# A top-k threshold search on two engines: three counting rounds for four, from a first guess computed on TensorE

## What is computed

```python
x = x + tanh(g_xattn) * attention(layernorm(x), ctx, ctx, Wq, bq, Wk, bk, Wv, bv, Wo, bo)
x = x + tanh(g_ffn) * ffn_fp8(layernorm(x), kernel, scales, bias)
# attention, 16 heads, d = 16:
Q = (q @ Wq.T + bq).reshape(b, h, s, d)      # a head is 16 tokens x 16 feature groups
scores = einsum('bhqd,bhkd->bhqk', Q, K) / sqrt(d)
topk_scores, topk_idx = top_k(scores, 64)    # 64 of 256 keys per row
probs = softmax(topk_scores)
out = einsum('bhqk,bhqkd->bhqd', probs, gather(V, topk_idx)) @ Wo.T + bo
```

## Time and profile before

| | |
|---|---|
| median of 3 runs | 3270.99 us (3270.64 to 3272.13) |
| the profiled execution | 3268.81 us, of it 3266.9 us span |
| ACT busy | 2730.3 us, 84% |
| DVE busy | 2691.6 us, 82% |
| PE busy | 1780.4 us, 54% |
| POOL busy | 966.1 us, 30% |
| tiles selected again by `settle` | 7 |

### The profile page before, as it was taken

How to read it: one execution, slowest core, us unless ns; L and a number is a source line. 1 busy time by engine, 2 the same in 40 slices (tenths; PEclk the granted TensorE clock), 3 DMA queues, 4 the chain that set the end, 5 groups by cost and what they waited for, 6 DMA issues and landing times.

```text
span 3266.9 us, 51511 instructions
## 1 busy us (share of the span) xinstructions
PE 1780.4 (54%) x7952; PEld 950.5 (29%) x7952; DVE 2691.6 (82%) x11883; ACT 2730.3 (84%) x9638; POOL 966.1 (30%) x1174
## 2 busy tenths in 40 slices
PE   3245555555465555455556556564556556454555
PEld 2122233332233233232323333332233223232222
DVE  1678888888888888888888888888888888888884
ACT  1888888998788898797889998988798788997983
POOL 5122223233222233232233223333223233232112
PEclk8567677777677777776667777767676767777777
DMA  4223332223333223331233333223333133331211
GB/s 70 38 43 60 49 47 52 52 49 63 52 52 54 45 49 63 52 55 34 48 64 56 60 48 56 48 48 64 53 49 55 33 62 61 55 54 33 40 24 46
DMA packets 451902, 166.43 MB, mean 51 GB/s; under 512 B 245616, under 2 KB 451440, under 8 KB 451520
## 3 DMA queue, kind: packets, MB, share of 16 engines
q1 hardware_dynamic: 451136, 162.38, 28.4%
q0 software_dynamic: 384, 0.33, 0.1%
HBM read 102.57 MB, written 59.24 MB: 50 GB/s over the span
## 4 chain that ended last, share of the span: by engine, by line
DVE 36%; ACT 30%; issue 17%; PE 14%; DVEq 2%; POOL 1%; ACTq 0%; DMA 0%; SPq 0%; POOLq 0%; another core or an unknown queue 0%
ACT act_junk L880 22%; DVE masked L1151 5%; DVE score_sb L1047 4%; PE ps_o L731 4%; DVE following L1157 4%; DVE masked L1146 3%; ACT unfit L891 3%; ACT pT_sb L900 2%; PE ps_a L684 2%; DVE X L1083 2%; PE ps_b L675 2%; PE ps_e L712 1%; PE ps_a L686 1%; DVE chord L1115 1%; PE ps_e L716 1%
## 5 line engine op out<-in xcount | busy, mean ns | idle before, releaser
L880 ACT ACTIVATE act_junk<-score_sb,X 128x256 int8<-128x256 f32 x3840 | 1892.1, 503 | 211.3 <-DVE X L1121 183.2
L712 PE MATMUL ps_e<-qs,ks 99*128 99x256 bf16 x1024 | 348.2, 350 | 1321.7 <-ACT pT_sb L900 1321.7
L731 PE MATMUL ps_o<-pT_sb,v_aug 128*32 128x256 f32 x2048 | 766.4, 514 | 0.5 <-ACT pT_sb L900 0.5
L880 ACT ACTIVATION_READ_ACCUMULATOR act_junk<-score_sb,X 128x1 f32 x3840 | 755.0, 197 | 0.0
L891 ACT ACTIVATE unfit<-score_sb,thr 128x256 bf16<-128x256 f32 x1024 | 463.1, 504 | 218.0 <-DVEq L1241 214.6
L1047 DVE TENSOR_SCALAR_CACHE_REDUCE score_sb<-ps_s 128x256 f32<-128x256 f32 x1024 | 418.8, 415 | 142.1 <-PE ps_s L698 140.0
L712 PEld LDWEIGHTS ps_e<-qs,ks 99*128 99x128 bf16 x1024 | 121.9, 119 | 1403.6 <-ACT unfit L891 1199.5
L1146 DVE TENSOR_SCALAR_CACHE_REDUCE masked<-score_sb,X 128x256 f32<-128x256 f32 x1024 | 426.3, 472 | 19.1 <-DVE x_res L1294 8.4
L1157 DVE MAX8 following<-masked 128x8 f32<-128x256 f32 x1024 | 357.7, 409 | 1.7 <-issue 0.7
L540 POOL CAST split<-proj 128x512 bf16<-128x512 f32 x64 | 48.0, 750 | 1042.8 <-ACT proj L866 1027.2
L716 PE MATMUL ps_e<-dropb,unfit 128*128 128x128 bf16 x2048 | 355.9, 273 | 0.0
(11 more groups left out here) (158 smaller groups left out, 3332.8 us busy)
## 6 DMA issues: line engine op xcount, KB each, us to landing
rows<-q_scr SPq DMA_DIRECT2D x192, 128.0 KB, 5.1
rows<-k_scr SPq DMA_DIRECT2D x192, 128.0 KB, 5.0
o_scr<-o_sb SPq DMA_DIRECT2D x128, 128.0 KB, 2.7
q_scr<-split SPq DMA_DIRECT2D x32, 384.0 KB, 2.7
k_scr<-split SPq DMA_DIRECT2D x32, 384.0 KB, 2.7
x_in<-in_x SPq DMA_DIRECT2D x32, 256.0 KB, 3.1
ctx_sb<-in_ctx SPq DMA_DIRECT2D x32, 256.0 KB, 2.7
v_scr<-proj SPq DMA_DIRECT2D x32, 256.0 KB, 5.8
```

Source lines behind the costliest of these rows:

```text
L712: nc.tensor.matmul(ps_e[:, n % 2, kc * TOK:(kc + 1) * TOK], ks[u][:, h, 8 * kc:8 * kc + 8, :].rearrange("d j t -> d (j t)"), qs[u][:, h, : ...
L731: ins = nc.tensor.matmul(ps_o[32 * c:32 * c + 32, half * TOK:(half + 1) * TOK], v_aug[p][:, 2 * h + kc, :], pT_sb[:, n % 2, kc * TOK:(kc + ...
L880: ins = nc.scalar.activation(act_junk[:, t, :], score_sb[:, slot, t, :], ACT.Sign, scale=-1.0, bias=X[slot % 2][:, 0, t:t + 1], accum_out= ...
```

## The change

It alters four things together.

1. **First guess.** DVE sums the keys and their squares (`sum_keys`; the squares come from POOL), PE turns the sums into a mean and a mean square for each head and dimension (`key_moments`), DVE makes weights of them (`weigh_keys`), PE multiplies the queries with these weights (`gauss`, 16 small matmuls for each group), ACT squares and copies the result (`evacuate_gauss`), and DVE takes X = mean + 0.6745 x deviation. The square root is an approximation on the bits.
2. **Rounds.** Three instead of four. ACT counts all 16 tiles.
3. **Finals.** Of 16 tiles, 4 (tiles 4, 5, 10, 11) are counted by ACT (`final_counts`, behind its guide counts); DVE masks those four one by one (L1309) rather than counting them and masking them four at a time.
4. **Heads per round.** With three rounds, ACT does heads (0, 1, 2), (3, 4, 5), (6, 7) in them, and DVE copies the same heads' scores.

The core of the diff, shortened:

```diff
-GUIDES = 4
-ACT_TILES = 15
+GUIDES = 3
-START = 0.25
-SLOPE = 0.0040 / 2
+START = 0.6745
+SLOPE = 0.0115 / 2
+WIDE = ((0, 1, 2, 3), (6, 7, 8, 9), (12, 13, 14, 15))
+NARROW = ((4, 5), (10, 11), ())
+HEADS = ((0, 1, 2), (3, 4, 5), (6, 7))
...
+                nc.gpsimd.tensor_tensor(rest[:], proj[1][:], proj[1][:], ALU.mult).then_inc(s_sq, 1)
...
+            def final_counts(i, slot, r, counted):
+                act.wait_ge(s_fin, FINAL * i + 1)
+                act.wait_ge(s_cnt, counted)
+                for t in NARROW[r]:
+                    ins = nc.scalar.activation(act_junk[:, t, :], score_sb[:, slot, t, :], ACT.Sign, scale=-1.0,
+                                               bias=X[slot % 2][:, 0, t:t + 1], accum_out=final_count[:, t:t + 1])
+                ins.then_inc(s_fc, 1)
+            def evacuate_gauss(i):
+                act.wait_ge(s_gs, i + 1)
+                act.wait_ge(s_st, at(3 * i))
+                act.wait_ge(s_fin, at(FINAL * (i - 2)))
+                both = ps_b[:, 0:(D + 1) * GT].rearrange("p (t d) -> p t d", d=D + 1)
+                nc.scalar.activation(gauss_sq, both[:, :, 0:D], ACT.Square)
+                nc.scalar.copy(gauss_mean[:], both[:, :, D]).then_inc(s_ge, 1)
...
             def start_thresholds(i, slot):
                 dve.wait_ge(s_copied, GH * i + GH)
                 carry(dve)
+                dve.wait_ge(s_ge, i + 1)
+                carry(dve)
...
-                nc.vector.tensor_scalar(x[:, 0, :], mx[:, slot, :], START, None, ALU.mult).then_inc(s_thr, 1)
+                nc.vector.tensor_reduce(variance[:], gauss_sq, AX.X, ALU.add).then_inc(s_st, 1)
+                root(sd[:], variance[:]).then_inc(s_st, 1)
+                nc.vector.scalar_tensor_tensor(x[:, 0, :], sd[:], START, gauss_mean[:], ALU.mult, ALU.add).then_inc(s_st, 1)
...
+                    for k, t in enumerate(narrow):
+                        nc.vector.scalar_tensor_tensor(masked[:, k, :], score_sb[:, slot, t, :], X[slot % 2][:, 0, t:t + 1],
+                                                       score_sb[:, slot, t, :], ALU.is_le, ALU.mult).then_inc(s_fin, 1)
...
-                nc.vector.tensor_tensor(unsure_b[:], s64[:], s65[:], ALU.is_le).then_inc(s_flag, 1)
+                nc.vector.scalar_tensor_tensor(unsure_b[:], s65[:], 0.0, s64[:], ALU.max, ALU.is_ge).then_inc(s_flag, 1)
...
                         for jh in range(2):
                             next(ending, None)
-                            if has(1) and not last:
-                                copy_scores(i + 2, fresh, 2 * r + 1, jh)
+                            if not last:
+                                copy(HEADS[r][2], jh)
                             next(steps, None)
```

More of the change, by code:

```diff
@@ L151, in build @@
         listed_i = sb("listed_i", [1, GT + 1], I32)
+        gauss_sq = place[:].bitcast(BF16)
+        gauss_mean = sb("gauss_mean", [P, GT])
+        variance = sb("variance", [P, GT])
+        spread = [sb(f"spread{k}", [P, GT]) for k in range(2)]
+        pick_dims = sb("pick_dims", [P, D])
+        key_sums = sb("key_sums", [P, 2, EC, NJ])
+        key_stats = sb("key_stats", [D, 2 * NJ])
+        key_var = sb("key_var", [D, NJ])
+        gauss_w = sb("gauss_w", [D, NJ, D + 1], BF16)
         ones_c = sb("ones_c", [P, 1])
@@ L820, in batch @@
                             out_project(b - 2, 2 * b + 1)
+                        if has(1) and n == 5:
+                            gauss(b + 1, (u + 1) % OPS, g, 2 * b + 6 if has(2) else 2 * NB,
+                                  2 * b + 4 + 2 * g if has(2) else 2 * NB)
+                        if has(2) and (g, n) == (1, 7):
+                            key_moments(b + 2)
             schedule(pe, batch)
@@ L946, in batch @@
                             guide_counts(2 * b + g + 1, (2 * p + g + 1) % RING, r)
-                        for n in (2 * r, 2 * r + 1):
+                        if NARROW[r]:
+                            final_counts(2 * b + g, 2 * p + g, r, GUIDES * (2 * b + g + 1) + (r + 1 if guided else 0))
+                        if has(1) and (g, r) == (0, 0):
+                            evacuate_moments(b + 1)
+                        if has(1) and r == GUIDES - 1:
+                            evacuate_gauss(2 * (b + 1) + g)
+                        for n in HEADS[r]:
                             if mixes:
@@ L962, in batch @@
                                 evacuate_ffn(b - 3)
+            evacuate_moments(0)
+            for g in range(2):
+                evacuate_gauss(g)
             for r in range(GUIDES):
@@ L1155, in final_tiles @@
                 carry(dve)
-                for k, t in enumerate(tiles):
+                for k, t in enumerate(wide):
                     nc.vector.max(following[:, t, 1:], masked[:, k, :]).then_inc(s_fin, 1)
+                yield
+                base += 2 * QUARTER + 1
+                if narrow:
+                    dve.wait_ge(s_fin, base)
+                    carry(dve)
+                    for k, t in enumerate(narrow):
+                        nc.vector.scalar_tensor_tensor(masked[:, k, :], score_sb[:, slot, t, :], X[slot % 2][:, 0, t:t + 1],
+                                                       score_sb[:, slot, t, :], ALU.is_le, ALU.mult).then_inc(s_fin, 1)
@@ L1299, in _ @@
             front_moments(1)
+            sum_keys(0)
+            weigh_keys(0)
             for i in range(2):
@@ L1335, in batch @@
                             convert_unsure(i - 1)
-                        if has(1):
-                            copy_scores(i + 2, fresh, 2 * r, 1)
-                        next(finals, None)
+                        copy(HEADS[r][0], 1)
+                        next(finals)
                         if r == 0 and mixes:
                             settle(i - 1, mixed)
-                        last = r == GUIDES - 1
+                        if has(1) and (g, r) == (0, 0):
+                            weigh_keys(b + 1)
+                        if has(2) and (g, r) == (1, 2):
+                            sum_keys(b + 2)
+                        next(finals)
+                        copy(HEADS[r][1], 0)
+                        copy(HEADS[r][1], 1)
+                        next(finals, None)
                         if last and has(1):
-                            for jh in range(2):
-                                copy_scores(i + 2, fresh, 2 * r + 1, jh)
                             start_thresholds(i + 2, fresh)
```

217 lines of the change are left out of this document (161 added, 56 removed).

## The result

The changed kernel takes 3369.54 us (median of 4, 3366.05 to 3371.54) against 3271.25 (median of 4) before: ratio 1.0299, 95% interval 1.0281 to 1.0317, so 98 us or 3.0% slower. Forecast was 3343 us, range 3285 to 3405. The profiled execution took 3371.54 us.

What follows compares the result with a forecast made beforehand. Each round was taken as bound by the later of two paths, ACT's counts and heads or DVE's finals, extras and update. From the 3271.0 us median, -19 for the rounds and +91 for settled tiles gave 3343 us, range 3285 to 3405.

Steps and rivals of the forecast that it cites:

- the five signs: In the changed profile: 15 settling runs, ACT 78 us, L1000 waiting 4 us, score waits over 140.0, clean batch 92.5 to 94.
- Settled tiles: Tiles settled after the rounds: 15 in 12 groups by float32 replay, 179 us against 88 for 7 before, +91 us.
- What the engines are spared: Work per batch: ACT 6.8 us less, DVE 5.1 us less; the ceiling of the gain, the order deciding how much shows.
- The first new wait: ACT's copy of four mixed heads waits for PE's mixing stage behind head 3: 2.1 us, 4.2 for the two groups.
- The second: Score copy ahead of the write of X, rounds 0 and 1, waits on PE; value projection 7.1 us in first group's round 0.
- The six rounds: A batch's rounds, each between ACT's first counts: 18.3, 17.0, 12.4 in the first group, 17.0, 16.1, 12.4 in the second.
- The sum: Six rounds make 93.2 us a batch against 93.8 before: -0.6 us, -19 us over 31 batches.
- The first (rounds pay in full): Rival: ACT's new waits fall into time it would wait for X anyway; a batch falls 5.1 us, 3204 us; chance 0.07.
- The second (7 tiles): Rival: the new guess settles as few tiles as before, some 7, giving 3252 us; chance 0.04.
- The third: Rival: chain of X longer than laid out, rounds 0 and 1 each 0.5 us more, batch 95.2, 3405 us; chance 0.16.

Runs made afterwards that it cites:

- after_none: Changed kernel with its last comparison turned so that no tile is ever marked unsure and the settling block never runs: 3185.2 us, ratio 0.9736.
- after_few: Changed kernel with other constants alone (START 0.68, SLOPE 0.0116 / 2), instructions the same, 6 settled tiles: 3258.3 us, ratio 0.9953.
- four_rounds: Changed kernel with the new first guess but four rounds of two heads, one final count on ACT in each round: 3576.3 us, ratio 1.0925.
- copy_late: Changed kernel with ACT's copy of the second half of the mixed values issued behind head 5's masks instead of head 4's: 3347.8 us, ratio 1.0226.
- before_none: Kernel before the change with its comparison for unsure rows given a bound no row meets, so no tile is settled: 3185.0 us, ratio 0.9734.

## Why the prediction was right

**Direction and cause.** Right: the range and the sign held, and the loss is that of the settled tiles, as forecast. Of the five signs four came: 16 settled tiles for 15, ACT busy 77.5 us in a clean batch for 78, the wait of L1000 of 4.5 us a batch for 4, and longer waits for scores than the 140.0 of before. The fifth did not: a batch of `after_none` is 95.5 us on average, not 92.5 to 94.

**Settled tiles, forecast +91.** Measured +98.2. The replay gave 15 tiles in 12 groups and 15 to 17 with noise; the chip settled 16 in 13. The prices of 12.6 and 9.4 us were 3% and 9% above the 12.2 and 8.6 that the three runs give. The replay is no oracle, though: for the constants of `after_few` it gave 3 and the chip 6, for `four_rounds` none and the chip 1.

**What the engines are spared, forecast -6.8 on ACT and -5.1 on DVE.** Measured over the two kernels without settling: -6.4 and -3.5. DVE's miss of 1.6 us is more than covered by the three instructions of the last step (165.0 against 62.6 us, 3.3 us a batch), which I had not seen coming; I had asked what the new square on POOL and the narrow masks would meet, not what the shifted round would.

**The first new wait, forecast 2.1 us twice a batch.** Measured 65 times 2.2 us, 4.5 us a batch on average. But its price on the path was not 4.2 us: `copy_late` got 22 us back for it, 0.7 a batch.

**The second, forecast through PE's 7.1 us.** Right in kind, and it is the wait that costs: 158.3 of 258.7 us for head 2 of the first group. That ACT's copy of the projection would wait too (140.5 us) I had not written down.

**The six rounds, forecast 18.3, 17.0, 12.4, 17.0, 16.1, 12.4.** Medians: 21.5, 16.9, 12.0, 17.3, 16.6, 11.9. Five are right to 0.5 us; the first is the term that was mis-sized, by 3.2 us. I worked out 18.9 and took 18.3, counting on a faster PE. In the batch shown above the round takes 21.5 us: PE needs 9.1 from the mixing stage to the scores (2031.96 to 2041.06) where I had 7.1, and the pieces before and behind it 0.6 more than laid out. The row I used was of a batch in which PE's clock rose during the projection; in half of the batches after the change it does not. There the round lasts 21.9 us in the median, in the other half 19.6 (13 batches each), so a slow PE explains most of the miss and a rest of 1.3 us stands without it.

**The sum, forecast -0.6 us a batch, -19 in all.** Measured +0.1 in all. That is near by luck, for two errors offset each other: the six rounds are 95.5 us long on average (all but the first and last three batches of `after_none`), 2.3 over my 93.2, and the kernel before (`before_none`) has 95.4 there, not the 93.8 of the one batch I took as typical. (The lower end of the range is 3288 us by its own terms, not 3285.)

**Rivals.** The first (rounds pay in full) stayed out, as its own test says: 6.4 us less work on ACT gave nothing. The second (7 tiles) did not occur; `after_few`, with 6, gave 3258.3, some 3270 with a seventh at 12.2, against the 3252 worked out for it. The third asked for 0.5 us more in four rounds, 95.2 us a batch; there was 3.2 us in one round, and the 95.5 us of a batch is nearer to its figure than to my 93.2. That the time came out 36 us under its 3405 is owed to the 95.4 of before, which it did not foresee either.

## What to carry to other kernels

Where three engines hand work round in written order and none is over 86% busy, an engine's spared work is worth what is left when the next one is late, here nothing of 6.4 us. Price a wait by taking it away: of two that each cost ACT 4.5 us a batch, one was worth 0.7 us, and the stage of the other 2.7 once it was moved to where no threshold waits behind it. Take the length of a batch from the mean of many; the one batch that looked typical was 1.6 us short of it. When an instruction is moved out of a collision, look in the new trace for what the other engine meets instead. And where a kernel falls back on a slow path for rare data, count how often it does before and after; here 9 tiles of 1024 were 3% of the time.

## What the runs showed of the hardware

The granted clock of TensorE, at a place that bound the batch. Windows of the changed kernel in its first round, then of the kernel before at the earlier trace rows:

```profile
2032.00:2041.60 9.60, 9.60 (x25) 4.89 (x26) 3.46 (x18) 2.87 (x7) 0.00 (x0) 0.50 0.00 1
```

```profile
1881.60:1889.20 7.60, 7.60 (x28) 4.05 (x29) 6.83 (x22) 7.60 (x30) 5.25 (x9) 0.68 0.02 3
```

PE had idled 6.49 and 7.14 us before the two. In the first it stayed at 0.50, its level of 1.2 GHz, through the projection, which lasted 6.31 us; in the second it rose on the way (mean 0.68; the first four matmuls of the projection took 2.08 us, the next four 1.13), and the projection lasted 4.35. From the first matmul of the projection to the next scores, 15 of 30 take 6.31 us after the change and 7 of 30 before, the others 3.5 to 4.5 (the first two batches left out). So a chain that runs through a PE that has waited pays some 2 us here when the clock stays down.
